# Emptying the cross-query projection's banks on ScalarE instead of VectorE in a fused decoder layer

## The reference

```
x = layernorm(x + self_attention(x))
q = (x @ Wq.T + bq) * (1 / sqrt(32))      # the cross query, scaled
x = layernorm(x + cross_attention(q, ctx))
x = layernorm(x + feed_forward(x))
```

## Time and profile before

| | us |
|---|---|
| median of 3 runs (lowest to highest) | 2428.76 (2426.14 to 2428.95) |
| the profiled execution: its own time / its span | 2426.63 / 2424.8 |
| PE busy over the span | 2358.7 (97%) |
| DVE, ACT, POOL busy | 1535.0 (63%), 1333.4 (55%), 1361.8 (56%) |
| PE by the chain that ended last | 74% |
| the C stage with its neighbours, roughly | 340 to 514 of the span |

### The profile page before, as it was taken

One profiled execution on the slowest core, in us unless ns is written; L12 is line 12 of the kernel. 1 busy time (PEld: TensorE's weight loads), 2 busy tenths in 40 slices (PEclk: granted clock), 3 DMA queues, 4 the chain that ended last, 5 costly groups with the idle time before them and its releaser, 6 DMA issues.

```text
span 2424.8 us, 58663 instructions
## 1 busy us (share of the span) xinstructions
PE 2358.7 (97%) x21644; PEld 2044.4 (84%) x21644; DVE 1535.0 (63%) x2621; ACT 1333.4 (55%) x3325; POOL 1361.8 (56%) x1189
## 2 busy tenths in 40 slices
PE   7999978999999999999999999999999899999999
PEld 7888847888888888888888888888888698998998
DVE  6666678846677666666666667677676724435342
ACT  5878852126666666666666666666666651221311
POOL 5777653346767657667567666667665533333332
PEclk9999979999999999999999999999999999999999
DMA  5444467636776677677777776776677831101010
GB/s 154 133 127 119 108 166 266 253 114 170 195 199 189 190 201 202 186 194 196 190 205 198 182 204 191 197 198 189 188 196 204 236 111 65 42 24 65 0 40 23
DMA packets 248846, 382.69 MB, mean 158 GB/s; under 512 B 114428, under 2 KB 124156, under 8 KB 248572
## 3 DMA queue, kind: packets, MB, share of 16 engines
q1 hardware_dynamic: 223996, 328.74, 47.8%
q10 hardware_dynamic: 24576, 50.36, 8.1%
HBM read 125.70 MB, written 39.32 MB: 68 GB/s over the span
## 4 chain that ended last, share of the span: by engine, by line
PE 74%; DVE 1%; issue 1%; SPq 1%; DMA 1%; POOL 1%; ACT 0%; ACTq 0%; DVEq 0%; POOLq 0%
PE D_ps_p L68 41%; PE D_ps_s L1881 7%; PE D_ps_p L1908 6%; PE E_ps_g L68 6%; PE E_ps_u L68 6%; PE E_ps_d L68 5%; PE E_ps_y L68 3%; SPq L1301 1%; DVE D_columns L1685 0%; PE E_ps_t L1934 0%; ACT D_e L1550 0%; DMA D_pT<-D_turned 0%; DMA E_w_int<-in_w_gate 0%; DVE D_turned L1699 0%; POOL E_acts_low L1473 0%
## 5 line engine op out<-in xcount | busy, mean ns | idle before, releaser
L1413 POOL TENSOR_SCALAR D_e<-D_e,D_columns 128x722 f32<-128x722 f32 x256 | 538.9, 2105 | 467.9 <-DVE D_columns L1691 467.9
L1550 ACT ACTIVATE D_e<-D_ps_s,D_columns 128x723 f32<-128x723 f32 x512 | 438.3, 862 | 389.8 <-DVE D_columns L1685 345.4
L1685 DVE TENSOR_REDUCE D_columns<-D_ps_s 128x1 f32<-128x723 f32 x512 | 439.5, 899 | 294.9 <-PE D_ps_s L1881 294.7
L1699 DVE STREAM_TRANSPOSE D_turned<-D_e 128x768 f32<-128x768 f32 x512 | 496.0, 972 | 19.0 <-DMA D_pT<-D_turned 18.4
L68 PE MATMUL D_ps_p<-D_ctx_high,cross_wk_high 128*128 128x362 f32 (+1 forms) x1024 | 350.1, 342 | 2.9 <-DVEq L1711 1.4
L68 PE MATMUL D_ps_p<-D_ctx_low,cross_wk_high 128*128 128x362 f32 (+1 forms) x1024 | 336.6, 329 | 0.0
L68 PE MATMUL D_ps_p<-D_ctx_high,cross_wk_low 128*128 128x362 f32 (+1 forms) x1024 | 334.8, 327 | 0.0
L68 PE MATMUL D_ps_p<-cross_wv_high,D_ctx_high 128*128 128x512 f32 (+1 forms) x656 | 259.7, 396 | 0.0
L68 PE MATMUL D_ps_p<-cross_wv_high,D_ctx_low 128*128 128x512 f32 (+1 forms) x656 | 259.3, 395 | 0.0
L68 PE MATMUL D_ps_p<-cross_wv_low,D_ctx_high 128*128 128x512 f32 (+1 forms) x656 | 257.7, 393 | 0.0
L1557 ACT ACTIVATE D_e<-D_e,D_columns 128x722 f32<-128x722 f32 x256 | 230.9, 902 | 10.4 <-DVE D_columns L1691 10.4
(11 more groups left out here) (254 smaller groups left out, 5265.9 us busy)
## 6 DMA issues: line engine op xcount, KB each, us to landing
D_pT<-D_turned SPq DMA_DIRECT2D x1536, 96.0 KB, 2.6
D_pT<-D_turned ACTq DMA_DIRECT2D x512, 96.0 KB, 2.7
D_craw<-in_ctxT SPq DMA_DIRECT2D x124, 361.0 KB, 3.5
self_v<-wstage SPq DMA_DIRECT2D x25, 256.0 KB, 2.4
A_v<-self_v SPq DMA_DIRECT2D x32, 200.0 KB
self_o<-A_o SPq DMA_DIRECT2D x32, 200.0 KB, 3.7
x<-C_x SPq DMA_DIRECT2D x5, 1280.0 KB, 8.0
cross_q<-C_qo SPq DMA_DIRECT2D x20, 320.0 KB, 4.2
```

Source lines behind the costliest of these rows:

```text
L1413: pool.tensor_scalar(head, head, inv[:, 2 * (s % 2):2 * (s % 2) + 1], None, ALU.mult)\
L1550: act.activation(e[n // 2 % 2][:, n % 2, 0:PARTS * PART].rearrange("p (a c) -> p a c", a=PARTS), parts_of(n), ACT.Exp, bias=neg_max[:, n % ...
L1685: dve.tensor_reduce(neg_max[:, n % 4:n % 4 + 1], parts_of(n), AX.XY, ALU.max, negate=True)\
L1699: dve.transpose(turned[quad % 2][:, :, 2 * (s % 2) + h, :].rearrange("p j (t r) -> p t j r", r=32), e[s % 2][:, h, :].rearrange("p (t j r) ...
```

## The change

ACT empties the query banks in place of DVE. It computes scale * bank + scaled bias with one activation (Identity, with the bias as a column per partition); the scaled bias is computed once, at the first unit, from the loaded one. DVE keeps what stood between the units, under the name `beside_q`. In ACT's stream `scale_q(g)` stands behind `high_x1(g, i)` and `high_o(g + 2, i)` of the same g and ahead of everything that came next. The last group's `high_x1` moves into `scale_q(3)`, each behind the unit at which PE turns that tile.

```diff
@@ names and buffers @@
-        bo_b, bq_c = out_sb("bo_b", [P, D]), out_sb("bq_c", [P, KD])
+        bo_b, bq_both = out_sb("bo_b", [P, D]), out_sb("bq", [P, 2, KD])
+        bq_c, bq_s = bq_both[:, 0, :], bq_both[:, 1, :]
@@ ACT @@
+                def scale_q(g):
+                    for u in range(QU):
+                        n = QU * g + u
+                        act.wait_ge(q_done, n + 1)
+                        if n == 0:
+                            act.wait_ge(b_loaded, 32)
+                            act.activation(bq_s, bq_c, ACT.Copy, scale=ISQ).then_inc(bq_scaled, 1)
+                            act.wait_ge(bq_scaled, 1)
+                        if u == 0:
+                            wait(act, q_stored, 64 * g)
+                        act.activation(qo[:, u // 2, u % 2 * HALF:(u % 2 + 1) * HALF], ps_q[u % 4][:, 0:HALF],
+                                       ACT.Identity, bias=bq_s[:, u // 2:u // 2 + 1], scale=ISQ).then_inc(qf_done, 1)
+                        if u in TURN_AFTER and g + 2 == NG:
+                            high_x1(NG - 1, TURN_AFTER[u])
...
                 for g in range(NG):
-                    for i in range(TT):
-                        high_x1(g, i)
+                    if g + 1 < NG:
+                        for i in range(TT):
+                            high_x1(g, i)
                     if g + 2 < NG:
                         for i in range(TT):
                             high_o(g + 2, i)
+                    scale_q(g)
                     if g == 0:
                         act.wait_ge(b_freed, 1)
                         act.wait_ge(pv_done, B)
                         c_high(act, [2, 3])
...
@@ DVE @@
-                def scale_q(g):
+                def beside_q(g):
                     for u in range(QU):
-                        n = QU * g + u
-                        dve.wait_ge(q_done, n + 1)
-                        if u == 0:
-                            wait(dve, q_stored, 64 * g)
-                        dve.tensor_scalar(qo[:, u // 2, u % 2 * HALF:(u % 2 + 1) * HALF], ps_q[u % 4][:, 0:HALF],
-                                          bq_c[:, u // 2:u // 2 + 1], ISQ, ALU.add, ALU.mult).then_inc(qf_done, 1)
                         if u in TURN_AFTER and g + 2 < NG:
                             low_o(g + 2, TURN_AFTER[u])
...
-                    scale_q(g)
+                    beside_q(g)
                     if g == 0:
                         c_low(dve, [2, 3])
```

More of the change, by code:

```diff
@@ L292, in phase_self_attention @@
         q_done, qf_done = sem("C_q_done"), sem("C_qf_done")
-        q_stored = sem("C_q_stored")
+        q_stored, bq_scaled = sem("C_q_stored"), sem("C_bq_scaled")
         int_loaded, int_max = [sem(f"C_int_loaded{j}") for j in range(3)], sem("C_int_max")
@@ L427, in _ @@
                           .then_inc(b_loaded, 16)
-                        sp.dma_start(bq_c[:, :], bq).then_inc(b_loaded, 16)
+                        sp.dma_start(bq_c, bq).then_inc(b_loaded, 16)
                         first_x(0)
```

## The result

The changed kernel takes 2434.67 us (median of 12 runs, 2431.73 to 2440.1), the kernel before beside it 2428.86 (12 runs, 2424.24 to 2434.35). The ratio is 1.0029, 95% interval 1.0021 to 1.0036: slower by 7.0 us, between 5.1 and 8.7. The forecast was +8.2 us and 2435.9.

A forecast was written before the change was run, and what follows sets the result against it. PE, busy 97% of the span, was taken as the bound. Terms -1.1 + 7.4 + 1.9 = +8.2 us on 2427.7 gave 2435.9 us; the range took in 2431.7 to 2438.6.

The forecast's parts named there:

- Part 1: Moving forty query bank evictions from DVE to ACT: 0.52 us each, PE waits for no bank, cost 0.
- Part 2: Group 0 and the weights' split: DVE reaches group 1's first turned tile sooner, gain 1.1 us.
- wait of 1.3: PE's wait for DVE's low part of a turned tile in group 1, forecast to shrink to 0.3 us.
- the 1.0: PE's other wait for DVE's low part of a turned tile, 1.0 us, forecast to stay.
- upper bound of 2.3: Most to be won in group 0: both PE waits for DVE's low parts go, 1.3 + 1.0 us.
- Part 3: Boundary between the two blocks: context's split stands behind the fortieth eviction, second block's first memset 7.4 us later.
- Part 4: PE's clock behind the longer boundary wait: half speed for 4.8 us, net +1.9 us.
- Rival (a): Boundary moves, but the clock's loss does not reach the end: +6.3 us, 2434.0 us; chance 0.14.
- Rival (b): Block boundary does not move, only group 0's gain of 1.1 us is left: 2426.6 us; chance 0.04.
- Rival (c): ACT late inside a group, waiting for a load, so evictions behind it stop PE: some 2442 us; chance 0.04.

The follow-up runs named there:

- first experiment: Changed kernel with ACT's four high parts of the context's split put between the first four evictions of the last group: 2427.32 us, ratio 0.9996 to the kernel before.
- third experiment: Changed kernel with ACT's eight high parts of cross_wk and cross_wv put ahead of group 0's evictions: 2433.85 us, one run.
- second experiment: Kernel before, DVE still emptying the banks, with ACT's context split made to wait for the fortieth query unit: 2436.95 us, ratio 1.0038.
- sixth experiment: Changed kernel with the context's four high parts behind evictions five to eight of the last group: 2430.05 us, ratio 1.0007 to the kernel before.
- fourth experiment: Changed kernel with 32 further matmuls, result unread, on PE behind the last query unit: 2431.94 us, one run.

## Why the prediction was right

**Part 1, the evictions on ACT: right.** One takes 529 ns (0.52 taken), 0.43 us from start to start (0.42 taken: 514.48 to 514.91), and no wait of PE names C_qo. The scaled bias delayed the first eviction by 0.23 us, not by 0.5, under the same cover. In the first experiment the move costs nothing that its interval can show. By the formula of the Trainium skill ("ScalarE: Activation LUTs", What ACT_TABLE_LOAD costs) this form is estimated at 547 ns; the runs have 18 ns less.

**Part 2, group 0: right.** DVE's way from the eighth eviction to the first turned tile of group 1 fell from 6.95 us to 5.90 (405.24 to 411.14). It fell no further because DVE, now early, waits 3.96 us for ACT's first high part:

```profile
406.32 2.50 DVE L114 TENSOR_TENSOR cross_wk_low<-wstage,cross_wk_high 128x512 fp32r<-128x512 f32 x4 [3.96 <-ACT cross_wk_high L107]
...
411.14 0.68 DVE L791 TENSOR_TENSOR C_x1s_low<-A_ps_s,C_x1s_high 128x512 fp32r<-128x512 f32 x1
```

1.1 us as forecast, with the wait of 1.3 shrunk to 0.3 and the 1.0 left. The upper bound of 2.3 was too low: the third experiment won 2.9 against before (110.30 to 107.38), because the two waits cost more than their idle time (2.9 us for 2.3 idle, by the distances given with that experiment).

**Part 3, the boundary: right.** The distance from eviction to memset grew by 7.18 us, where 7.4 was the sum. Of the missing 0.2, 0.16 are POOL's four parts, 6.71 us in place of 6.87. The second experiment makes this loss alone, the sixth makes a part of it.

**Part 4, PE's clock: the mechanism right, the size off.** The term was 4.8 us at half speed, 2.4 lost, 0.5 hidden, net 1.9. In the changed kernel's profile it was 1.3 net (4.71 to 6.02), from 4.3 us of low clock; in the second and third experiments 2.1 (6.79 and 6.86). So it is no fixed price: for nearly the same wait, 8.6 to 8.9 us, the low clock lasted 4.3 us once and 6.1 and 6.2 in the two others. What decides that is open. The prediction also took from one profile that a wait of 2.56 us leaves the clock up; that does not hold in others, as the last section shows. Also the matmuls of the keys took 0.30 us from start to start at the low clock and 0.167 at full, 1.8 times as long and not twice. One profile does not give the mean of such a term.

**The sum.** -1.1 + 7.2 + 1.3 = +7.4 in the profile, +7.0 by the ratio, +8.2 forecast. Rival (a), no loss by the clock at the end, is refuted by the changed kernel's own profile (0.50 behind the gap, 6.02 us in place of 4.71) and by the rest of the span, in which no wait is seen to make it good. The measured +7.0 alone would not refute its +6.3. The fourth experiment shows the loss gone with the wait. Rival (b) needed ACT to start the parts by 506.2, and they started at 514.91. With the order repaired it is what the first experiment shows: -1.1 by its distances, 0.9996 by its time. Rival (c) did not come; its nearest relative is told below. Its price was also added wrongly: four groups at 1 to 3 us are 4 to 12 us and not 4 to 9.

## What to carry to other kernels

When work moves to another engine, look at what stands behind it in that engine's program order, not only at the engine's free time: ACT had room for forty evictions, but work that had been done early in its idle time now stood behind the last of them, and a second engine's work behind that. A barrier turns such a tail into time for everyone, plus what PE's clock loses behind a long wait. The repair is one of order: put the work that others wait for between the evictions, where the engine idles anyway.

## What the runs showed that I had not expected

ACT's first eviction of group 4 waited for a store, which DVE's did not in the kernel before:

```profile
503.18 0.53 ACT L627 ACTIVATE C_qo<-A_ps_s,C_bq 128x320 f32<-128x320 f32 x1 [2.25 <-DMA cross_q<-C_qo]
```

It must not overwrite the result of group 3 before SP's last store of it has landed. In the kernel before, DVE was busy with its search for the largest integer from 499.57 on, came to this eviction at 502.12 and did not wait. The 2.25 us are hidden by the four banks, since PE waits for none. I had written that the stores of q keep their times, and had not asked whether the new engine would meet them.

And the length of PE's wait alone does not tell whether its clock falls. A wait of 3.6 us at the boundary was followed by the low clock (sixth experiment), and one of 2.56, ahead of the first query unit, was not in the kernel before. But that same wait of 2.56 us stands in all eight profiles, in work that no edit touched. In four of them (before, changed, second, third experiment) the clock behind it was 1.00, in the four others 0.50. The sixth experiment's, with the stretch behind it (PEclk 0.50):

```profile
361.54 0.77 PE L68 MATMUL A_ps_a<-self_wo_high,C_o_high 128*128 128x512 f32 x1 [2.56 <-DVE C_r L777]
```

```profile
361.54:362.50 0.96, 0.96 (x2) 0.80 (x3) 0.77 (x3) 0.00 (x0) 0.00 (x0) 0.50 0.00 0
```

What decides between them is open. It is one source of the differences between executions whose work is the same up to there, and a forecast can give such a term only as a range.
